# A two-layer post-norm network on one NeuronCore: table multiplications in two of TensorE's waits, and a small ScalarE copy ahead of its first

## What is computed

```python
x = L0_attn_x
x = _layernorm(x + _L0_attn_ref(x, L0_attn_past_kv, L0_attn_W_qkv, L0_attn_gn_weight, L0_attn_gn_bias), axis=-1)
x = _layernorm(x + _L0_ffn_ref(x, L0_ffn_W_fc, L0_ffn_ln_w, L0_ffn_ln_b, L0_ffn_W_proj), axis=-1)
x = _layernorm(x + _L1_attn_ref(x, L1_attn_Wq, ...), axis=-1)
x = _layernorm(x + _L1_ffn_ref(x, L1_ffn_w_router, L1_ffn_wi, L1_ffn_wo), axis=-1)
```

```python
router_probs = jax.nn.softmax(router_logits, axis=-1)
gate, idx = jax.lax.top_k(router_probs, K)
mask = jax.nn.one_hot(idx, E, dtype=jnp.float32)
pos = jnp.cumsum(mask_kt, axis=1) * mask_kt - 1.0
disp_k = jax.nn.one_hot(pos, C, dtype=jnp.float32) * mask[..., None]
```

## Time and profile before

| what | value |
|---|---|
| time, median of 3 runs | 923.56 us (922.23 to 925.37) |
| profiled execution, span from first to last instruction | 923.6 us |
| TensorE busy | 826.7 us, 90% of the span, 8838 instructions |
| VectorE busy | 614.9 us, 67% |
| ScalarE busy | 481.8 us, 52% |
| GpSimd busy | 254.6 us, 28% |
| data moved | 79.56 MB |

### The profile page before, as it was taken

The page is one execution under the profiler, slowest core; times in us unless marked ns, Lnnn a source line. Parts: engine busy times, 40 slices in busy tenths (PEclk is TensorE's granted clock), DMA queues, the critical chain, the costliest instruction groups (busy, mean ns, idle before and its releaser), DMA issues. The chain is left out here.

```text
span 923.6 us, 23206 instructions
## 1 busy us (share of the span) xinstructions
PE 826.7 (90%) x8838; PEld 688.1 (75%) x8838; DVE 614.9 (67%) x1408; ACT 481.8 (52%) x999; POOL 254.6 (28%) x323
## 2 busy tenths in 40 slices
PE   5999999998899999998999889889989839999960
PEld 4788888887677777766777778777667729999960
DVE  2578787878547777777565425677776875756626
ACT  2444444443777777766954324544654224445325
POOL 1156664221202222223000000004232131656344
PEclk9999999999999999999999989999989769999985
DMA  8500000000000000002476344435222212656439
GB/s 309 184 25 17 23 17 23 17 11 2 1 1 1 1 2 1 1 1 70 139 194 189 99 111 114 117 89 178 92 93 92 92 29 84 161 160 190 122 50 344
DMA packets 76429, 79.56 MB, mean 86 GB/s; under 512 B 22592, under 2 KB 66496, under 8 KB 75968
## 3 DMA queue, kind: packets, MB, share of 16 engines
q1 hardware_dynamic: 71376, 72.36, 25.5%
q0 software_dynamic: 3968, 5.25, 3.3%
q10 hardware_dynamic: 1008, 0.91, 0.3%
HBM read 50.71 MB, written 27.79 MB: 85 GB/s over the span
## 5 line engine op out<-in xcount | busy, mean ns | idle before, releaser
L713 DVE TENSOR_TENSOR r_prob<-r_pS,const 128x512 f32<-128x512 f32 x128 | 82.0, 682 | 25.1 <-PE r_pS L540 25.1
L1089 DVE SCALAR_TENSOR_TENSOR f_gl<-att_res,small_first,f_gh 128x512 fp32r<-128x512 f32 x64 | 47.3, 748 | 37.2 <-ACT f_gh L1014 34.7
L943 PE MATMUL f_pY<-wpjT,f_gh 128*128 128x256 f32 x256 | 66.1, 292 | 0.3 <-DVE f_gl L1089 0.3
L944 PE MATMUL f_pY<-wpjT,f_gl 128*128 128x256 f32 x256 | 63.4, 281 | 0.0
L1349 PEld LDWEIGHTS q_bank<-q_xT,att_res 128*64 128x64 f32 x1024 | 55.6, 137 | 7.2 <-issue 4.2
L943 PEld LDWEIGHTS f_pY<-wpjT,f_gh 128*128 128x128 f32 x256 | 48.7, 190 | 15.9 <-issue 13.4
L2426 POOL DMA_INDIRECT sum_dram<-e_yo,y_id x24 | 43.1, 1795 | 63.1 <-ACT e_yo L2559 47.4
L1349 PE MATMUL q_bank<-q_xT,att_res 128*64 128x128 f32 x1024 | 59.2, 274 | 0.0
L1008 ACT ACTIVATE att_res<-f_pH 128x512 f32<-128x512 f32 x64 | 38.0, 594 | 40.1 <-PE f_pH L928 39.4
L2540 ACT ACTIVATE e_hh<-e_pH 128x320 fp32r<-128x320 f32 x64 | 26.2, 433 | 55.3 <-PE e_pH L2465 55.0
L839 POOL TENSOR_SCALAR t_ey<-t_es 128x8 f32<-128x8 f32 x4 | 0.8, 202 | 195.0 <-ACT t_sqrow L1911 195.0
(11 more groups left out here) (307 smaller groups left out, 2363.2 us busy)
## 6 DMA issues: line engine op xcount, KB each, us to landing
kv_dram<-att_res SPq DMA_DIRECT2D x32, 256.0 KB, 3.7
t_ring<-kv_dram SPq DMA_DIRECT2D x128, 64.0 KB, 2.3
wi<-L_ffn_wi SPq DMA_DIRECT2D x8, 1024.0 KB
wo<-L_ffn_wo SPq DMA_DIRECT2D x8, 1024.0 KB
x_res<-L_attn_x SPq DMA_DIRECT2D x8, 512.0 KB, 5.1
q_dram<-att_res SPq DMA_DIRECT2D x8, 512.0 KB, 3.1
t_q<-q_dram SPq DMA_DIRECT2D x64, 64.0 KB, 2.8
x_dram<-x_res SPq DMA_DIRECT2D x8, 512.0 KB, 3.0
```

The costliest lines, as they stand in the source:

```text
L713: dve.tensor_tensor(prob[t % 2][:, r, :, :], pS[r][:, :, :], dec[:, r, :, :], ALU.mult)\
L943: pe.matmul(out, gh[c % 4][:, cols], net.wpjT[:, c, :], start=(c == 0 and t % 2 == 0), stop=False, skip_group_check=True)
L944: mm = pe.matmul(out, gl[c % 4][:, cols], net.wpjT[:, c, :], start=False, stop=(c == NH - 1), skip_group_check=True)
L1089: dve.scalar_tensor_tensor(out=gl[c % 4][:, :], in0=g[c][:, :], scalar=net.lnw[:, c:c + 1], in1=gh[c % 4][:, :], op0=ALU.mult, op1=ALU.sub ...
```

## The change

The edits stand in four places. A helper `keep_turning` multiplies a 128x128 table by itself, repeated to 512 columns, into a bank, a given number of times; nobody reads the result.

1. GpSimd clears one more small buffer, `spin` (128x128, bf16), behind the value buffers, and adds to `cleared`. TensorE waits for that behind its first projection and then multiplies `spin` 4 times into `pRR`.
2. ScalarE copies one column of a cleared value buffer onto itself, in front of its first `take` and behind the three waits that stood there.
3. TensorE multiplies the bf16 table of ones into `pH[1]`: 14 times behind `ids(0)`, 14 times behind `count(1)`, 20 times behind `ids(1)`.
4. TensorE multiplies the f32 table of ones once into `pD[1]`, behind the first expert's `front`.

```diff
--- before.py
+++ after.py
@@ -207,10 +207,18 @@
         self.pkv_raw = first["pkv"].rearrange("p (k e) -> p k e", k=KD)
         self.raw = self.room[:, KD * 3 * DIM:KD * 3 * DIM + 2 * KD * HID].rearrange("p (j n) -> p j n", j=2)
         self.u_both = early("u_both", [P, 2, DIM])
+        self.spin = early("spin", [P, P], BF16)
         self.u0, self.u1 = (self.u_both[:, i, :] for i in range(2))
 
 
 PIECE = KD * HID // (2 * TPB)
+
+
+def keep_turning(pe, bank, of, times):
+
+    moving = of.rearrange("p (a n) -> p a n", a=1).broadcast_to([P, TPB, P])
+    for _ in range(times):
+        pe.matmul(bank, of, moving, start=True, stop=True, skip_group_check=True)
 
 
 def retention(net, lasting, ctx):
@@ -375,6 +383,7 @@
         for i in range(TPB):
             ins = pool.memset(vO[i][:, :], 0.0)
         ins.then_inc(cleared.sem, 1)
+        pool.memset(net.spin[:, :], 0.0).then_inc(cleared.sem, 1)
         pool.wait_ge(c0_in.sem, c0_in.after(16))
         for t in range(TPB):
             decay_queries(0, t)
@@ -481,6 +490,7 @@
         act.wait_ge(c0_in.sem, c0_in.after(16))
         act.wait_ge(cleared.sem, cleared.after(1))
         act.wait_ge(zeroed.sem, zeroed.after(1))
+        nc.scalar.activation(vO[0][:, 0:1], vO[0][:, 0:1], ACT.Copy)
         take(0, 0)
         batch(0, False, True)
         with act.Fori(1, BATCH - 1) as b:
@@ -652,6 +662,8 @@
                         turn_back(b - 1, j, 4 * (b * TPB + t) + 1 + j % 2)
 
         project(0, 0)
+        pe.wait_ge(cleared.sem, cleared.after(2))
+        keep_turning(pe, pRR[:, :], net.spin[:, :], 4)
         batch(0, False, True)
         mean_magnitudes()
         with pe.Fori(1, BATCH - 1) as b:
@@ -1864,8 +1876,11 @@
         turn_x(BATCH - 1, 1)
         logits(BATCH - 1)
         ids(0)
+        keep_turning(pe, pH[1], ones[:, :], 14)
         count(1, BATCH)
+        keep_turning(pe, pH[1], ones[:, :], 14)
         ids(1)
+        keep_turning(pe, pH[1], ones[:, :], 20)
 
     def heads_of(u, r):
 
@@ -2515,6 +2530,7 @@
             turn_back(e)
 
         front(0, 0)
+        keep_turning(pe, pD[1][:, :], net.table["ones"], 1)
         pe.wait_ge(d_act.sem, d_act.after(0))
         for c in range(EARLY):
             up(0, 0, c)

TensorE's order at the start of the first phase, before. Names behind the arrow are operands; `[waits ...]` lists the semaphores of the first instruction of a row.

```order
L512 MATMUL r_pQV<-r_xT,w_first 128x128 [waits r_x_in0,r_w_in]
L512 MATMUL r_pQV<-r_xT,w_first 128x128 x3
L515 MATMUL r_pQV<-w_first,r_xT 128x256 x2
L525 MATMUL r_pKK<-r_xT,w_first 128x128 x4
L512 MATMUL r_pQV<-r_xT,w_first 128x128 [waits r_qv_taken,r_x_in1]
L512 MATMUL r_pQV<-r_xT,w_first 128x128 x3
```

## The result

The changed kernel takes 918.93 us, median of 19 runs (916.25 to 922.31), against 923.74 us for the kernel before in 19 runs beside them (920.14 to 927.87). The ratio of the paired runs is 0.9953, with a 95% interval from 0.9941 to 0.9964. By this ratio the change takes off 4.3 us, between 3.3 and 5.4; the two medians are 4.8 us apart. The change makes the kernel faster, by more than the 0.3% that can be told from nothing.

A forecast was written before the change was run, and what follows sets the result against it. TensorE was taken to bound the kernel, losing time to clock dips around waits. Start -3.1 and seam -2.0 gave -5.1 us, from 923.6 to 918.5 us; range 916.8 to 923.0.

The forecast's parts named there:

- The table load: Start, ScalarE: the new copy brings the table load forward, so the first real copy starts 1.30 us earlier.
- The clock over the second projection: Start, TensorE: the clock stays up through the second projection after a shorter, half-filled wait; gain 1.82 us, between 0 and 1.82.
- The third projection waits for its tile: Start: third projection would start at 17.07, its input tile lands by 17.13 at worst; some 0.1 us lost.
- The start's sum: First layer: table load and second projection's clock together 3.12 us, less some 0.1 lost to a load; -3.1 us.
- The groups of 14: Routing seam: both groups fill TensorE waits; first group costs 0 if the count is quick, and gains nothing.
- The place matmuls: Seam, behind the third table: 32 matmuls VectorE awaits go from 1.47 to 0.87 us; -0.6 us.
- The barrier: Seam's end, where stages change: the last 20 fillers take 4.7 us, barrier no later, about 1 us to spare.
- The slower rival: Seam: fillers outlast their waits at the lower clock; about +4, 927.9 us, deciding once 20 take over 5.7; chance 0.07.
- Transposes: First transposes of the experts, behind the barrier: from 1.90 to 1.16 us; -0.7 us.
- expert matmuls: First expert's first twelve matmuls: from 3.28 to 1.76 us; -1.5 us.
- The reserve of 0.8 us: Seam: terms sum to 2.8 us but only -2.0 counted, for remaining idleness and one relapse of 0.7 or 1.5.
- half of it: Rival: table load gained (-1.3), but the clock mostly unchanged or less costly typically (about -1); near 921.3 us; chance 0.24.

The follow-up runs named there:

- copy_only: The kernel before with the small ScalarE copy alone, no added matmuls; 921.91 us, ratio to before 0.9979.
- minimal: The changed kernel without the four start multiplications and both groups of 14, and with 12 in place of 20; 918.99 us, ratio to before 0.9944.
- no_c: The changed kernel without the last 20 multiplications, those behind `ids(1)`; 920.28 us, ratio to before 0.9969.
- start_both: The kernel before with the ScalarE copy and the four start multiplications, nothing in the seam; 922.00 us, ratio to before 0.9970.
- gap_fill: The changed kernel with six more multiplications in TensorE's wait at the end of the first batch entry; 919.43 us, ratio to before 0.9953.
- c12: The changed kernel with 12 multiplications in place of the last 20 in front of the barrier; 919.04 us, ratio to before 0.9959.
- no_one: The changed kernel without the single f32 multiplication behind the first expert's `front`; 920.83 us, ratio to before 0.9972.
- seam_only: The kernel before with the 48 seam multiplications and the one f32 multiplication, nothing at the start; 922.15 us, ratio to before 0.9984.

## Why the prediction was right, and where it was not

The forecast was 918.5 us, the median is 918.93; the range and the side hold. By its own steps:

**The table load: -1.30 us predicted, right.** The first copy starts 1.47 us earlier in the change and 1.39 in `copy_only`; the rest over 1.30 is not in my sum. In the three traces without the copy the table load starts 0.18 to 0.19 us behind the end of the projection's values; in the eleven with it the first real copy starts 0.03 to 0.05 us behind that same end. So the load costs 1.45 us there: its 1.30 and a start that is 0.15 us later. I had also read that ScalarE was idle until the load; it issued transfers until 5.8 us, and with the copy the load stands right behind them, which costs nothing. The drain that the Trainium skill (ScalarE: Activation LUTs, "What ACT_TABLE_LOAD costs") adds would have made it 2.66 us; no run of this case shows it, and in the trace of before the ScalarE work that stands ready behind the later loads starts 1.29 to 1.30 us after them as well.

**The clock over the second projection: -1.82 predicted, -1.65 measured; the mechanism was half right.** I put it down to a short wait of which half is filled. The short wait alone does it (`copy_only`, `minimal`). The number could not show this, since with the copy there both explanations give the same gain; that it came out is no credit to the filler. I had also priced the four fillers at nothing with the full clock and 0.6 us with the lower, and that was too kind: whether the clock rises before or behind them is a matter of a few tenths of a us. In the change it rose in time. In `no_c`, with the same start, it did not:

```profile
12.39 1.47 PE L221 MATMUL r_pRR<-spin 128*128 128x512 bf16 x4
13.70 1.05 PE L522 MATMUL r_pQV<-r_xT,w_first 128*128 128x128 f32 x8
```

The fillers begin at 12.39, run slow at first, and hold the second projection back to 13.70, though ScalarE's first copy was as early as ever (10.93). `copy_only` with the same late rise starts it at 12.98. From ScalarE's first copy to the second projection the two traces without these fillers (`copy_only`, `minimal`) and five of the nine with them need 1.86 to 1.87 us; the other four, all with a late rise (turned keys 1.54 to 1.92 us), need 2.00, 2.36, 2.68 and 2.77. The fillers at the start thus cost between 0 and 0.9 us and earn nothing beside the copy.

**The third projection waits for its tile: 0.1 us predicted, right.** It started at 17.21 against a forecast of 17.07. The wait did turn into one for a load, by the weight load ahead of it:

```profile
17.21 0.97 PEld L522 LDWEIGHTS r_pQV<-r_xT,w_first 128*128 128x128 f32 x8 [0.21 <-DMA r_xT<-xT]
```

I had listed that as a sign of being wrong; it is worth 0.1 to 0.2 us. The start's sum of -3.1 is -3.12 in the profile and 2.8 us by `start_both` (1.1 to 4.4). The prediction also reads a dip at the start in the page's clock row; that row has none there, only the earlier trace rows show it.

**The groups of 14: cost 0, gain 0, right.** The first took 3.54 us, a little over its 3.2, since its head ran slow, and the count began 0.38 us behind it. VectorE's product kept its time in all traces: with the fast count and with the slow one of `minimal` it follows the last tokens' copy by 15.3 us.

**The place matmuls: -0.6 predicted, -0.25 measured.** This is a term that was mis-sized. I took the second 14 to carry the clock over the waits between the four parts. They end at 739.1, and the parts begin at 741.28, 742.59, 744.00 and 744.41; the clock held to 744.4 us and fell within the last part, as the starts show: 0.025 us from one to the next at 744.06, 0.04 at 744.96, and the window behind is 0.56. The wait of VectorE for it went from 0.96 us in the trace of before to 0.71:

```profile
752.65 0.17 DVE L2239 TENSOR_REDUCE m_idf<-t_pA 128x8 f32<-128x16 f32 x1 [0.96 <-PE t_pA L1818]
```

Of the nine traces with the second 14 it moved in four (6.63 to 6.75 us from the product: the change, `gap_fill`, `c12` and `no_c`) and stayed in five (6.87 or 6.88, as before).

**The barrier: "about 1 us to spare", wrong by 1.4.** I said that 20 fillers take 4.7 us. They took 5.86, since the clock had fallen just ahead of them, and they started at 745.04, not behind a gain of 0.6 us. The slower rival had said that it decides from 5.7 us on, where more than 5 of the 20 run at the lower clock. That point was passed: each slow one costs 0.2 us more, so 5.86 us instead of 4.5 (0.22 us apiece) are, by my estimate, six or seven slow ones. What saved the forecast is that it was a single late rise, for which the rival itself had a price of 1 to 2 us. The rows then waited for TensorE by 0.3 to 0.4 us, which I had named as a sign of being wrong as well. `c12` takes this back in its stretch; in its time it is not to be seen.

**Transposes -0.7 and expert matmuls -1.5, right:** -0.72 and -1.45, and `no_c` and `no_one` show that each hangs on its own filler. **The reserve of 0.8 us** that I kept for one relapse went to the two terms above (0.35 less at the place matmuls, 0.4 more at the barrier) in the place of a relapse; the sum of -2.0 is right by the profile, partly because one error covered the other: the reserve was kept for a relapse that did not come, and just as much was lost elsewhere. That is luck. By the times `seam_only` is worth 1.5 us, between 3.2 less and 0.2 more.

**The starting point.** I took the profiled execution as equal to the median because its span of 923.6 us is. In each of the runs since, the execution's time is 1.6 to 1.7 us above its span; so that execution was at about 925.3 us (an estimate; the slowest of the three runs was 925.37), 1.5 to 1.8 above the median. That is the likely reason why -5.1 by the profile became -4.3 by the clock: some of the dips that this profile shows are not in every execution. I had that as the "half of it" rival, and a small part of it came true.

## What to carry to other kernels

Where TensorE's granted clock falls because of a wait, first ask whether the wait can end earlier: one small ScalarE instruction that brings a table load forward was worth the load and the clock together, and made the fillers beside it useless. Fillers paid here only directly ahead of TensorE work that something waits for, and then in every link of the chain: 13 did what 53 did, as far as seven runs can tell, and leaving out a single one lost all of the expert matmuls' gain. In front of a barrier price them at the lower clock too, since past the end of the wait each is paid in full: forty of them gave back 3.9 us.

## What was unexpected in the hardware

The clock's rise during the first projection is not fixed. In the 14 traces the last eight of its matmuls (the turned keys) took 1.05 us in three, 1.11 to 1.54 in six and 1.90 to 1.92 in five, so it rose anywhere from ahead of them to behind them. The pace of the matmuls is all that shows this: the windows view prints a granted clock of 1.00 for these microseconds in every trace, also where the eight turned keys take 1.90 us and not 1.05, as in `copy_only`:

```profile
10.00:12.00 2.00, 2.00 (x9) 1.80 (x8) 0.00 (x0) 0.89 (x3) 0.00 (x0) 1.00 1.01 409
```

I go by the pace here: where the same view has 0.50, eight such matmuls also take 1.9 us (the second projection of before, 1.95). Whatever is put behind the first projection finds either level.

An idle stretch did not lower the clock at once, and work that had begun again did not stop the fall: in `no_one` the transposes ran at full speed at 755.27, TensorE idled for 1.99 us from 756.46, and the fall came at 758.5 to 758.9, when it was already working again. So a wait is paid by the work behind it. The place matmuls of the change show the same: they started fast at 741.28 after 2.23 us of idleness and ended slow.

A 128x512 multiplication by a bf16 table starts 0.22 us behind the one before it at the full clock (14 in 3.18 us, of which the last record alone is 0.38), and one with f32 operands 1.13 us in two records at the full clock and 2.07 at the lower.
